# The second layer's node tiles: eight of 512, eight of 256 and one of 128, in place of eleven, two and one

## The reference, cut to what matters

```python
x = x + _L0_gnn_ref(_layernorm(x), edge_weight1, ...)      # layer one
x = x + _L0_ffn_ref(_layernorm(x), ...)
x = x + _L1_gnn_ref(_layernorm(x), edge_weight, ...)       # layer two: gather and sum
x = x + _L1_ffn_ref(_layernorm(x), ...)                    # layer two: 8 experts, top 2

def _L1_gnn_ref(x, edge_vals, Wp, bp, W1, b1, W2, b2, src, dst):
    h = relu(x @ Wp.T + bp)                      # 128 features
    agg = segment_sum(edge_vals[:, None] * (h ** 2)[src], dst, N)
    return h @ W1.T + b1 + (agg ** 0.5) @ W2.T + b2

def _moe(tokens, router_w, w1, b1, w2, b2):      # layer two's experts, hidden size 256
    probs = softmax(tokens @ router_w.T)         # top 2 of 8, made to sum to 1
    out = tokens
    for e in range(8):
        h = gelu(tokens @ w1[e] + b1[e])
        out = out + combine[:, e:e + 1] * (h @ w2[e] + b2[e])
    return out
```

## Time and profile before

| | us |
|---|---|
| runs | 2799.94, 2797.59, 2789.29 |
| median | 2797.59 |
| the profiled execution, its own time | 2798.88 |
| its span in the trace | 2796.9 |
| PE busy | 2348.9 (84%) |
| POOL busy | 1676.3 (60%) |
| DVE busy | 1766.5 (63%) |
| ACT busy | 1134.1 (41%) |

### The profile page before, as it was taken

One profiled execution on the slowest core, in us unless ns is written; L12 is line 12 of the kernel. 1 busy time (PEld: TensorE's weight loads), 2 busy tenths in 40 slices (PEclk: granted clock), 3 DMA queues, 4 the chain that ended last, 5 costly groups with the idle time before them and its releaser, 6 DMA issues.

```text
span 2796.9 us, 47418 instructions
## 1 busy us (share of the span) xinstructions
PE 2348.9 (84%) x17989; PEld 1385.7 (50%) x17989; DVE 1766.5 (63%) x4319; ACT 1134.1 (41%) x1835; POOL 1676.3 (60%) x1678
## 2 busy tenths in 40 slices
PE   0137999999999999999999835588888888889997
PEld 0134555555555555555457724445444444444556
DVE  8475777767667777676666634355555655555665
ACT  4023444444444444444546601133333333333466
POOL 3677657566575565654430067777777777777730
PEclk9998999999999999999999955599999999999999
DMA  5633333233332333332220122122222222222210
GB/s 204 248 115 102 104 97 110 90 112 95 93 111 88 101 105 91 116 90 78 72 64 19 59 75 62 52 64 70 69 63 59 71 70 71 67 58 69 65 46 10
DMA packets 115790, 238.02 MB, mean 85 GB/s; under 512 B 30290, under 2 KB 69452, under 8 KB 115044
## 3 DMA queue, kind: packets, MB, share of 16 engines
q0 software_dynamic: 66560, 163.68, 21.1%
q1 hardware_dynamic: 48996, 71.26, 7.4%
HBM read 209.16 MB, written 25.67 MB: 84 GB/s over the span
## 4 chain that ended last, share of the span: by engine, by line
PE 51%; POOL 29%; issue 11%; DVE 5%; DMA 2%; ACT 1%; POOLq 0%; DVEq 0%; SPq 0%; ACTq 0%
POOL ring L592 29%; PE psY L716 19%; PE psH L685 18%; PE psE L667 4%; PE psM L780 3%; PE psC L692 1%; DMA ring<-table,src_s 1%; PE psM L732 1%; PE psM L740 1%; PE psE L671 1%; DVE t0st L907 1%; DVE hid L1280 1%; DVE hsc L1286 1%; PE psE L675 0%; PE psM L727 0%
## 5 line engine op out<-in xcount | busy, mean ns | idle before, releaser
L592 POOL DMA_INDIRECT ring<-table,src_s x1664 | 1646.7, 990 | 955.7 <-issue 637.6
L685 PE MATMUL psH<-xnT,wbuf 128*128 128x512 f16 (+2 forms) x4032 | 903.6, 361 | 1.5 <-ACT hid L1469 1.5
L716 PE MATMUL psY<-hsc,wbuf 128*128 128x512 f16 (+2 forms) x4032 | 892.4, 357 | 10.7 <-DVE acc L1119 6.8
L1469 ACT ACTIVATE hid<-psH,b,scl 128x512 f32<-128x512 f32 (+2 forms) x672 | 486.4, 724 | 958.0 <-PE psH L685 956.8
L1280 DVE TENSOR_TENSOR hid<-hid,psC 128x512 f32<-128x512 f32 (+2 forms) x672 | 416.4, 620 | 558.4 <-ACT hid L1469 332.4
L716 PEld LDWEIGHTS psY<-hsc,wbuf 128*128 128x128 f16 x4032 | 388.8, 99 | 416.9 <-issue 28.9
L685 PEld LDWEIGHTS psH<-xnT,wbuf 128*128 128x128 f16 x4032 | 373.1, 102 | 313.2 <-issue 33.0
L675 PE MATMUL psE<-ohbuf,ring 128*128 128x40 f32 x1664 | 259.4, 311 | 196.6 <-DMA ring<-table,src_s 196.0
L1286 DVE TENSOR_TENSOR hsc<-hid,hsc 128x512 f16<-128x512 f32 (+2 forms) x672 | 417.3, 621 | 0.3 <-ACT hsc L1477 0.3
L1477 ACT ACTIVATE hsc<-hid 128x512 f16<-128x512 f32 (+2 forms) x672 | 380.6, 566 | 12.4 <-DVE hid L1280 11.7
L675 PEld LDWEIGHTS psE<-ohbuf,ring 128*128 128x128 f32 x1664 | 237.5, 219 | 249.7 <-DMA ring<-table,src_s 238.8
(11 more groups left out here) (155 smaller groups left out, 1693.6 us busy)
## 6 DMA issues: line engine op xcount, KB each, us to landing
ring<-table,src_s POOLq DMA_INDIRECT x1664
wbuf<-w_in SPq DMA_DIRECT2D x2, 4096.0 KB, 20.9
wbuf<-x_in SPq DMA_DIRECT2D x7, 896.0 KB, 13.1
table<-ring SPq DMA_DIRECT2D x7, 896.0 KB, 3.6
feat<-table SPq DMA_DIRECT2D x11, 512.0 KB, 4.1
xin<-x_in SPq DMA_DIRECT2D x11, 512.0 KB, 3.8
x_d<-x SPq DMA_DIRECT2D x11, 512.0 KB, 3.1
xin<-x_d SPq DMA_DIRECT2D x11, 512.0 KB
```

Source lines behind the costliest of these rows:

```text
L592: pool.indirect_dma_start(out=l.ring[:, g % l.R, k, :], out_offset=None, in_=l.table, in_offset=bass.IndirectOffsetOnAxis(ap=src_s[:, c:c ...
L685: last = mm(psH[n % 2][:, 0:l.TT[t]], l.w1(e, i, k, c), x[:, j, k, 0:l.TT[t]], start=(k == 0 and m == 0), stop=(k == KD - 1 and m == 2))
L716: last = mm(psY[d][:, 0:l.TT[t]], l.w2(e, i, c, d), h[:, j, 0:l.TT[t]], start=False, stop=(n == l.M - 1 and m == 2))
L1469: f(hid[n % 4][:, 0:l.TT[t]], psH[n % 2][:, 0:l.TT[t]], (ACT.Relu, ACT.Gelu)[l.i], scale=l.un_up, bias=l.b1[:, n // l.HC, n % l.HC:n % l.H ...
```

## The change

One entry of a table: the tiles at the end of layer two's list.

```diff
 LAG = 2
-ENDS = (([], [2, 2, 1]), ([], [2, 2, 1]))
+ENDS = (([], [2, 2, 1]), ([], [2] * 8 + [1]))
 WACC = T + 256
```

## The result

The changed kernel takes 2763.6 us, the median of 4 runs (2762.7 to 2768.9), against 2796.6 for the kernel before in the same comparison: ratio 0.9886, 95% interval 0.9871 to 0.9901. It is 33 us faster. I had forecast 2779 with a range down to 2765, so the direction and the mechanism were right and the size was not: the profiled execution took 2763.81 us where the sum gave 2778.7, 14.9 us less.

The account below looks back on a forecast made before the run. POOL's gathers were taken to bound tiles 0 to 8, PE tiles 10 to 13. From tile 6's mark, 2329.7 + 61.9 + 54.2 + 244.7 + 86.2, plus 2.0 around the span, gave 2778.7, predicted as 2779 us; range 2765 to 2803.

Parts of the forecast that it names:

- step 3: Tiles 8 to 13, six of 256 nodes: 244.7 us together, 40.8 each, built from tile 11's 35.9 us.
- the start: Mark of tile 6 in layer two at 2329.72 us, up to which nothing changes there.
- the place of the handover: Kernel before: tiles 0 to 8 at POOL's pace, 10 to 13 at PE's, handover in tile 9 at 2599.62 us.
- the floor: POOL's gathers decide the narrow tiles: tile 14 can't start before about 2679 us, hence 2767; chance 0.13.
- Step 1: Tile 6 takes the order of tile 9 before: 66.2 - 1.0 - 3.3 = 61.9 us, bounds 61.9 to 65.2.
- Step 2: Tile 7 takes the order of tile 10 before: 54.2 us, so tile 8 starts at 2445.8.
- Step 4: Tiles 8 to 13: POOL needs 43.6 us a tile, PE 40.8; the lead of 5 groups (26 us) lasts.
- The fastest rival: Narrow tiles need less than 39 us, so POOL's gathers stay the bound: 2767 to 2770 us; chance 0.13.
- Step 5: From tile 14's start at 2690.5 to the end, same tiles and sums as before: 86.2 us.
- That the wait only moves: Narrow tiles' ACT and DVE chains make PE wait, 42.5 to 46 us a tile: 2789 to 2810 us; chance 0.24.
- That DVE's work falls on the chain: The 39 added groups' DVE work falls on the softmax chain and nearby steps: 2829 us; chance 0.09.
- That the clock stays low: PE at half clock through tiles 8 to 13, about 29 us more a tile: 2953 us; chance 0.02.

Follow-up runs that it names:

- The more gathers: The kernel before and the changed kernel, each with a fifth transfer for each group of layer two: 3035.0 us and 3028.8 us.

## Why the prediction was off

In short: the mechanism was right, and the step that failed is step 3, the term for the six narrow tiles, put at 244.7 us (40.8 a tile) and measured at 234.2 (39.0). Its 10.5 us and the 5.3 us of the start are the miss; the errors of the other terms nearly cancel.

*What bounds the kernel, and where it ends.* Right. PE left POOL's pace at tile 6, as said; gather waits fell by a third, as said; the place of the handover, the lead of POOL and the floor came out within 3 us (I had put the floor at a start of tile 14 of 2679; it started at 2677.6, and the gathers would have let it start some 1.5 us earlier). The more gathers bear out the condition on the lower level: gain 33 us at four transfers, 6 to 13 at five. On the upper level, where four gave no gain, three gave a loss.

*The start, 2329.7.* Off by 5.3 us: the mark lay at 2324.4. The second trace of the kernel before has it at 2325.3. I had one execution, 1.3 us above its median, and took its marks for the kernel's.

*Step 1, tile 6: 61.9.* Measured 64.8. The order was right and the wait came at the place named, 2.25 us and not 1.3, since the group came 9.6 us behind the tile's mark and not 8.3. And half of the 3.3 us of clock loss that I had taken away was there:

```profile
2334.03 1.09 PE L675 MATMUL psE<-ohbuf,ring 128*128 128x40 f32 x8 [2.25 <-DMA ring<-table,src_s]
2334.95 2.62 PE L685 MATMUL psH<-xnT,wbuf 128*128 128x512 f16 x6
2337.36 2.04 PE L716 MATMUL psY<-hsc,wbuf 128*128 128x512 f16 x6
2339.23 0.59 PE L780 MATMUL psM<-gnn_w,featT 128*128 128x256 f32 x2
```

From 2334.95 to 2339.23 are 4.3 us for twelve matmuls that take 2.6 when fast; 1.7 us lost.

*Step 2, tile 7: 54.2.* Measured 54.1.

*Step 3, the six narrow tiles: 244.7.* Measured 234.2; this is the term that failed, by its size. Its error has three parts. The largest is the clock. I had carried tile 11's loss behind its wait of 2.47 us (some 1.6 us, its clock being 0.95) into all six. Here are a tile that has it (10) and one that hasn't (9), both behind the same line 802:

```profile
2513.88 0.30 PE L802 MATMUL psM<-ident_b,c 128*72 128x128 bf16 x2 [2.36 <-DVEq L1263]
2514.02 0.82 PE L685 MATMUL psH<-xnT,wbuf 128*128 128x256 f16 x6
2514.68 0.82 PE L716 MATMUL psY<-hsc,wbuf 128*128 128x256 f16 x6
2515.43 0.28 PE L692 MATMUL psC<-cT,spread 24*128 24x256 bf16 x1
...
2553.10 0.30 PE L802 MATMUL psM<-ident_b,c 128*72 128x128 bf16 x2 [2.52 <-DVEq L1263]
2553.24 1.17 PE L685 MATMUL psH<-xnT,wbuf 128*128 128x256 f16 x6
2554.20 1.48 PE L716 MATMUL psY<-hsc,wbuf 128*128 128x256 f16 x6
2555.62 0.39 PE L692 MATMUL psC<-cT,spread 24*128 24x256 bf16 x1
```

From start to start, the first six matmuls take 0.66 us in tile 9 and 0.96 in tile 10, the next six 0.75 and 1.42. Four of the six tiles had a clock of 1.00, with waits of 2.36 to 2.52 us in them, so 4 x 1.6 = 6.4 us of cost weren't there. The tile with two sums had the loss in all three traces (11 before, twice, and 14 now, each at 0.95), the tiles with 8 or 9 sums in two cases of six. What decides it no run shows. Second, the wait at `psC` fell from 1.31 to between 0.40 and 0.49 in each tile, by the whole 0.87 that I had given as the bound and not by the half that I chose: 2.6 us. Third, the sums cost 0.81 us behind `psY` and 0.91 behind `psC`, which makes some 0.84 and not 0.87: 1 us. Together 10 us of 10.5. The waits at line 802 stayed at 2.36 to 2.52 as said, two more groups beside them: DVE's and PE's additions did cancel.

*Step 4.* POOL had 1.5 to 3 us to spare at the end: tile 13 summed groups 204 and 205 at 2667.9 and 2674.4, and their last transfers landed near 2666.4 and 2671.5 (counted back from the last issue at 2679.0 at 1.25 us a transfer, and 2.5 to land). The fastest rival, POOL as the bound, was nearly there. So PE's own sum and the formula of A give nearly the same time in this kernel, and the run with four transfers can't tell them apart.

*Step 5, the end: 86.2.* Measured 84.2, of which tile 15 (30.2 against 31.8) is the most, with its clock at 1.00. The kernel before had the same 30.2 in its second trace, so this too belongs to the execution.

The sum of the errors, -5.3 + 2.9 - 0.1 - 10.5 - 2.0 = -15.0, is the 14.9 us that were missing. *The range* went wrong at its lower end. I set it by POOL's floor, but counted that floor from the marks of the one execution and so left no room for an execution that starts tile 6 some 5 us earlier. With the old start the same trace would have ended at 2769, inside the range: step 3 made the forecast miss, and the start made the range miss.

*The rivals.* That the wait only moves: the narrow tiles do wait more, by 23 us at line 802 and `psC`, but these waits were in the sum. That DVE's work falls on the chain: it didn't. That the clock stays low: tiles 8 to 13 ran at 0.96 to 1.00, against 0.93 at POOL's pace. The Trainium skill ("TensorE: Matmul & The Clock Gate", "Why this matters for your kernels") advises to keep all dimensions at 512 or more. This trace agrees as far as narrow tiles do take longer (78.1 us a pair against some 67, the estimate above). But on the lower level the waits for gathers that fell away outweighed it.

## What to carry to other kernels

Where a fixed order meets a slow supplier, ask for each piece: when does it arrive, and how much other work stands behind it? The end is the largest of these sums, and moving the asking back by more, smaller tiles at the end of the list gains (work behind) - (pieces x pace), until the supplier's own end is the floor or the buffer between the two is full. Before trusting such a gain, check on more than one chip that the supplier is the bound there: here the gain was there on one level of two.

## What the runs showed of the hardware

- The same program took 2797 us on one chip and 3166 to 3196 on five others. In a trace from one of the five, matmuls start 0.7 us apart, or multiples of it, for some 12 us on end. POOL's pace of 1.25 us a transfer, where it doesn't wait, is the same in the traces of both levels. The cause is open.
- On the five chips tiles of 512 with 17 groups took 97 to 110 us with four transfers a group and 77 to 90 with three. No trace from these chips has a wait for a gather in those tiles.
- Equal waits of about 2.5 us were followed by a slower clock in some tiles (0.95 and 0.96) and not in others (1.00), within one execution. The same tile of the same kernel took 31.8 us at 0.95 in one execution and 30.2 at 1.00 in another.
